# Attention A with 128 stationary columns: GpSimd's norm behind the splits, and z, xn and the projections in slots 10 to 15 of the preceding iteration

## The chip, the core and the metric

The kernel runs on one core of one Trainium2 chip. The metric is the device time of one execution in microseconds (us); smaller is better. TensorE is called PE below, VectorE DVE, ScalarE ACT, GpSimd POOL, and the queue of SyncE that issues the DMAs SP.

## What is computed

A small transformer on 32 sequences of 256 tokens of width 128, float32: attention A, a feed-forward layer, attention B, the feed-forward layer again. The program has three stages one after the other, `attention_a`, `dense` and `attention_b`. The change is in `attention_a` alone, which computes, for each sequence (a block):

```python
y  = layernorm(x)                                # the caller's norm
z  = layernorm(y)                                # attention A's own norm, before g1 and b1
xn = z * g1 + b1
q, k = lin(xn, Wq, bq) / sqrt(8), lin(xn, Wk, bk)   # 16 heads of 8
v  = lin(xn, Wv, bv)                             # 8 "rules" of 8, shared by all heads
out  = softmax(q @ k.T) @ v                      # per head, 256 x 256 scores
comp = softmax over rules([qv, out] @ Ws.T + bs)
ao   = sum over rules(comp * out)                # goes to DRAM, and y too
```

The scores are taken from bfloat16 operands that carry float32 precision: q and k are each split into three bfloat16 parts, and the 9 products of parts are stacked on 72 rows of the contraction. The row maxima of the scores (negated, again in three parts) are stacked as 24 more rows, so that a second matmul of the same operands gives the scores shifted by their maximum, transposed.

## The kernel before

`attention_a` is a software pipeline written out by hand: every engine runs `body(j, u)` for the iterations n = 2j + u, and in iteration n an engine works on several blocks at once, each with its lag. `active(j, u, lag)` asks whether block n - lag exists. The first six iterations and the last are unrolled, the others are a hardware loop of two iterations. The engines meet through semaphores only, and each executes its instructions strictly in the order of the code. PE and ACT split an iteration into 16 slots `s` (one head each); the order inside a slot is that of the code.

In iteration n, with the lines of the profile:

- SP loads x of block n+2, stores y of block n (L286), stores the parts of block n as soon as POOL has split them (L292), waits until they have landed in DRAM, and reads them back in two halves of 8 heads as stacked operands `q_st[i]` (L305) and `k_st[i]` (L308, three per half). Each half also waits until the shift matmuls of block n-2 no longer read that half of the buffer (`shifted`): half 0 until slot 4, half 1 until slot 12.
- PE: in slot 1 it transposes z of block n (L628), in slot 3 it projects q and k of block n (L647, L648), in slot 5 it projects v of block n-1 (L652), in slots 2 and 10 it transposes parts of the row maxima (L639). Every slot has two *shift* matmuls (L593, block n-1 from slot 13 on, block n-2 before), four *values* matmuls (L609, each two records), and the 16 score units of block n-1 (L578, two matmuls each) are spread by `S_AT` over slots 0 to 13, two units in slots 0 and 2. A score unit writes one of two PSUM banks, so unit w waits until DVE has reduced unit w-2 (`maxed`); unit 0 waits for the stacked operands of its half to land (`stack_in`), and so does unit 8 in slot 6. In iterations 1 to 4, slot 0 opens with `fold`, the product of two feed-forward weights that a later stage needs (L557 to L563).
- The shift matmul of head 8 of block n-2 stands in slot 5, that of head 0 of block n-1 in slot 13; each waits (`m_in`) until POOL has written 8 heads' rows of maxima into `q_st` (`spread`, L345).
- ACT: slot 2 copies transposed maxima (L470) and makes xn of block n (L473), slot 4 evicts q and k of block n from PSUM (L477, L479), slot 10 copies maxima (L488). Every slot has an exponential (L496) and every odd slot a copy of values (L505); slot 5 has another exponential (L511). At the end of slot 14 it makes y of block n+1 (L520, twice) and z of its first half (L525), at the end of slot 15 z of its second half.
- DVE reduces the score units (L697), and between them does the weighing of block n-3 (L772 to L782), the moments of block n+1 (L727, L731), the sums of block n-4 (L740), and the splitting of the maxima (L714, L716).
- POOL, in this order: `spread(1, n-2)` (L345), the subtraction of block n-3 (L360), the four splits of block n (L376 to L379, which wait for `qk_d`, ACT's eviction of slot 4), the first four instructions of the norm of block n+1 (L395 to L398), `spread(0, n-1)` (L345), the other four of the norm (L403 to L406), the four products of block n-3 (L416).

The bank `zv_ps` takes in turn the transposes of z, the projection of v and the folds, the bank `qk_ps` the projections of q and k and the transposed maxima (`mt_ps`); semaphores guard each reuse.

## Time and profile before

| | |
|---|---|
| median of 3 runs | 1583.43 us (1572.7 to 1587.1) |
| the profiled execution | 1586.89 us |
| its span | 1585.1 us |
| mean granted TensorE clock over the span | 0.933 |
| `attention_a` | from 0 to about 772 us of the span |
| its iterations, its blocks | n from -1 to 35, 32 |

The profile is of one execution. A row of the timeline is one instruction, or a run of equal ones where it ends in x2 or more; the bracket at its end tells how long the engine had been idle before it, and what ended that. Matmuls overlap, so the start of the next says more than the duration.

### The profile page before, as it was taken

What the parts mean: (1) busy time and instruction counts of PE and PEld (TensorE: products, weight loads), DVE (VectorE), ACT (ScalarE), POOL (GpSimd) and SP (SyncE); (2) the same over time, 40 slices, a digit from 0 to 9 for tenths busy, and PEclk for the clock granted to TensorE, in tenths of its full rate; (3) what the DMA queues carried; (4) which work ended last, traced back from release to release, by engine and by line L of the source; (5) the groups of instructions that cost most, each with busy time, mean ns of one, the idle gap of its engine ahead of it and who ended that gap; (6) DMA issues with size and microseconds to landing.
All of it is one profiled execution on the core that took longest, in us unless ns stands there. A gap on an engine that the chain in (4) does not pass through costs nothing. (4 is left out here: it accounts for less than half of the span.)

```text
span 1585.1 us, 52984 instructions
## 1 busy us (share of the span) xinstructions
PE 1328.7 (84%) x16996; PEld 1165.0 (73%) x16996; DVE 1095.4 (69%) x3074; ACT 873.5 (55%) x2020; POOL 927.5 (59%) x1340
## 2 busy tenths in 40 slices
PE   5999999999999999999477873787887778887786
PEld 4898998899888988999456652576666667666675
DVE  4467787788777887888344444667677777767874
ACT  2466766666666666676356652444454544444442
POOL 4456766667667666775478873445445554444551
PEclk9899999999999999999789995879799998879996
DMA  4523322332233223331144422434344444334331
GB/s 136 159 85 104 101 77 82 89 99 80 79 89 99 78 81 89 99 91 51 44 127 121 134 70 74 111 109 119 105 127 119 116 121 124 106 104 117 112 117 46
DMA packets 181701, 158.23 MB, mean 100 GB/s; under 512 B 12529, under 2 KB 163185, under 8 KB 181618
## 3 DMA queue, kind: packets, MB, share of 16 engines
q1 hardware_dynamic: 181618, 157.17, 35.1%
q8 instruction: 46, 0.75, 0.2%
q14 instruction: 37, 0.30, 0.1%
HBM read 113.09 MB, written 44.04 MB: 99 GB/s over the span
## 5 line engine op out<-in xcount | busy, mean ns | idle before, releaser
L609 PE MATMUL a_bank<-a_vp,a_prob 128*128 128x74 f32 x4096 | 598.0, 253 | 0.0
L609 PEld LDWEIGHTS a_bank<-a_vp,a_prob 128*128 128x128 f32 x4096 | 587.8, 192 | 5.5
L697 DVE TENSOR_REDUCE a_nmax<-a_bank 128x2 f32<-128x512 f32 x512 | 344.9, 685 | 156.9 <-PE a_bank L578 156.7
L496 ACT ACTIVATE a_prob<-a_bank 128x512 f32<-128x512 f32 x512 | 305.5, 597 | 216.0 <-PE a_bank L593 210.7
L578 PE MATMUL a_bank<-a_k_st,a_q_st 96*128 96x256 bf16 x1024 | 259.5, 276 | 38.3 <-DVE a_nmax L697 25.2
L593 PE MATMUL a_bank<-a_q_st,a_k_st 120*128 120x256 bf16 x1024 | 281.5, 275 | 2.2 <-POOL a_q_st L345 2.2
L416 POOL TENSOR_TENSOR a_prod<-a_ov,a_wgt 128x512 f32<-128x512 f32 x128 | 152.5, 1192 | 34.1 <-POOL a_prod L416 17.2
L345 POOL TENSOR_SCALAR a_q_st<-a_mt 24x2048 bf16<-24x2048 bf16 x64 | 121.5, 1898 | 82.6 <-ACT a_mt L470 36.9
L578 PEld LDWEIGHTS a_bank<-a_k_st,a_q_st 96*128 96x128 bf16 x1024 | 128.9, 134 | 50.0 <-DVE a_nmax L697 32.1
L1504 ACT ACTIVATE c_prob<-c_bank 128x256 f32<-128x256 f32 x256 | 98.8, 386 | 101.4 <-PE c_bank L1596 97.1
L593 PEld LDWEIGHTS a_bank<-a_q_st,a_k_st 120*128 120x128 bf16 x1024 | 140.1, 137 | 11.0 <-issue 2.6
L1647 PE MATMUL c_bank<-c_vb,c_prob 128*64 128x18 f32 x2048 | 109.3, 221 | 0.8 <-DVE c_ad L1919 0.8
L505 ACT COPY a_ov<-a_bank 128x292 f32<-128x292 f32 x256 | 101.5, 396 | 14.4 <-POOL a_prod L416 13.0
L1439 POOL TENSOR_SCALAR c_parts<-c_kq 128x512 bf16<-128x512 f32 x32 | 19.9, 621 | 147.9 <-ACT c_kq L1529 147.9
L1802 DVE TENSOR_REDUCE c_nmax<-c_bank 128x8 f32<-128x512 f32 x128 | 88.0, 687 | 20.6 <-PE c_bank L1616 19.4
L1574 PE MATMUL c_bank<-c_uv,c_skn 128*64 128x144 f32 x384 | 47.2, 326 | 63.9 <-DVE c_am L1840 62.8
L1647 PEld LDWEIGHTS c_bank<-c_vb,c_prob 128*64 128x64 f32 x2048 | 90.9, 151 | 7.2 <-issue 3.7
L1421 POOL TENSOR_SCALAR c_vb<-c_vs 64x128 f32<-64x128 f32 x128 | 39.0, 305 | 86.9 <-PE c_bank L1647 56.2
L1596 PEld LDWEIGHTS c_bank<-c_q_st,c_k_st 128*64 128x64 bf16 x2048 | 82.4, 121 | 6.7 <-issue 1.4
L1574 PE MATMUL c_bank<-c_late,c_pick 88*64 88x256 bf16 x512 | 80.3, 307 | 2.0 <-issue 2.0
L1596 PE MATMUL c_bank<-c_q_st,c_k_st 128*64 128x64 bf16 x2048 | 81.6, 204 | 0.0
L740 DVE TENSOR_REDUCE a_ao<-a_prod 128x128 f32<-128x1024 f32 x64 | 77.3, 1209 | 4.3 <-POOL a_prod L416 4.3
(205 smaller groups left out, 2821.2 us busy)
## 6 DMA issues: line engine op xcount, KB each, us to landing
a_q_st<-scratch_a_parts_dram SPq DMA_DIRECT2D x64, 288.0 KB
a_k_st<-scratch_a_parts_dram SPq DMA_DIRECT2D x192, 96.0 KB
c_q_st<-scratch_c_parts_dram SPq DMA_DIRECT2D x64, 288.0 KB
c_k_st<-scratch_c_parts_dram SPq DMA_DIRECT2D x192, 96.0 KB
scratch_a_parts_dram<-a_parts SPq DMA_DIRECT2D x32, 384.0 KB, 2.7
scratch_c_parts_dram<-c_parts SPq DMA_DIRECT2D x32, 384.0 KB, 2.7
a_x<-in_x SPq DMA_DIRECT2D x32, 128.0 KB, 3.5
scratch_y<-a_y SPq DMA_DIRECT2D x32, 128.0 KB, 3.1
```

What stands on the lines that cost most here:

```text
L345: pool.tensor_scalar(q_st[o][MROW:AROWS, hs, :], mt[half_][MROW:AROWS, :].unsqueeze(1).broadcast_to([AROWS - MROW, H // 2, T]), 1.0, 0.0, ...
L416: pool.tensor_tensor(prod[o][:, gs, :].rearrange("p g (e r) -> p g e r", r=R), ov[o][:, gs, 0:RD].rearrange("p g (e r) -> p g e r", r=R), ...
L496: act.activation(prob[h % 4][:, :, :].rearrange("p a b -> p (a b)"), t_ps[h % 2][:, :], ACT.Exp).then_inc(exped, 1)
L505: act.copy(ov[(i + lag) % 2][:, 4 * g:4 * g + 4, :], o_ps[g % 2][:, 0:4 * VC].rearrange("p (g c) -> p g c", g=4)[:, :, 0:CQ]).then_inc(ov_ ...
L578: mm = pe.matmul(s_ps[t][:, hh * T:(hh + 1) * T], q_st[o][0:MROW, 2 * g + hh, t * P:(t + 1) * P], k_st[o][0:MROW, 2 * g + hh, :], start=Tr ...
L593: mm = pe.matmul(t_ps[h % 2][:, c * T:(c + 1) * T], k_st[o][0:AROWS, h, c * P:(c + 1) * P], q_st[o][0:AROWS, h, :], start=True, stop=True)
L609: mm = pe.matmul(o_ps[g % 2][:, at:at + VM], prob[h % 4][:, c, t * P:(t + 1) * P], vp[o][:, c, 0:VM], start=c == 0, stop=c == NT - 1)
L697: dve.tensor_reduce(nmax[:, t, 2 * g:2 * g + 2, 0], s_ps[t][:, :].rearrange("p (h k) -> p h k", h=2), AX.X, ALU.max, negate=True).then_inc ...
L1504: act.activation(prob[g % 4][:, :], t_ps[g % 2][:, 0:T], ACT.Exp).then_inc(exped, 1)
L1574: mm = pe.matmul(out[cs, :], lhsT[:, cs], rhs, start=True, stop=True)
L1596: mm = pe.matmul(t_ps[g % 2][hh * SEG:(hh + 1) * SEG, cs], k_st[st][:, 2 * g + hh, cs], q_st[st][:, 2 * g + hh, cs], start=False, stop=Tru ...
L1647: mm = pe.matmul(o_ps[a * SEG:(a + 1) * SEG, at:at + VG], prob[g % 4][:, c * SEG:(c + 1) * SEG], vb[st][:, t, src:src + VG], start=True, s ...
```

## The change

On POOL the splits of block n come first in an iteration, ahead of `spread(1, n-2)` and the subtraction, and the eight instructions of the norm of block n+1 stand together ahead of `spread(0, n-1)`. What makes the input of the splits moves one stage back: in iteration n, block n+1 (not n) is transposed and projected. ACT makes y and z of block n+1 in slots 10 and 11 (before: 14 and 15), PE transposes z in slot 12 (before: slot 1 of the next iteration), ACT makes xn at the end of slot 13 (before: slot 2 of the next), PE projects q and k at the start of slot 15 (before: slot 3 of the next), and ACT evicts them first thing in slot 0 of the next iteration (before: slot 4 of it). Waits follow: the transposes of z wait for the newest v eviction (`v_d`), the projections for the newest copy of maxima of slot 10, the transposes of maxima of slot 2 (no longer those of slot 10) for the eviction of q and k, and a fold waits until xn has left the bank. No instruction is added or taken away apart from waits.

```diff
--- before.py
+++ after.py
@@ -220,6 +220,7 @@
         OFF, PVLAG = 13, 2
         S_AT = (0, 0, 1, 2, 2, 3, 4, 5, 6, 7, 8, 9, 10, 11, 12, 13)
         MT_AT = (10, 2)
+        Z_AT, ZT_AT, XN_AT, QK_AT = 10, 12, 13, 15
         PIECES, STAGES, FOLDED = 4, 5, 8
         N_LOAD, N_LOAD_V = 4, 8
         FOLD_AT = range(1, 1 + NG // 2)
@@ -350,6 +351,24 @@
             def body(j, u):
                 n = 2 * j + u
                 i = u
+                if active(j, u, 0):
+
+                    pool.wait_ge(qk_d, (n + 1) * 2)
+                    if not isinstance(j, int) or n >= 2:
+                        pool.wait_ge(parts_out, (n - 1) * 16)
+
+                    def split(k, ins):
+                        ins.then_inc(split_d, 1)
+                        pool.wait_ge(split_d, n * SPLIT + k)
+                        apart(pool, spare)
+
+                    apart(pool, spare)
+                    split(1, pool.tensor_scalar(parts[i][:, :, 0, :], qk[i][:, :, :], 1.0, 0.0, ALU.mult, ALU.add))
+                    split(2, pool.tensor_tensor(rest[:, :, :], qk[i][:, :, :], parts[i][:, :, 0, :], ALU.subtract))
+                    split(3, pool.tensor_scalar(parts[i][:, :, 1, :], rest[:, :, :], 1.0, 0.0, ALU.mult, ALU.add))
+                    split(4, pool.tensor_tensor(parts[i][:, :, 2, :], rest[:, :, :], parts[i][:, :, 1, :],
+                                                ALU.subtract))
+
                 if active(j, u, 2):
                     spread(1, n - 2, i)
                 if active(j, u, 3):
@@ -361,24 +380,6 @@
                                        cmax[:, :].unsqueeze(2).broadcast_to([P, H * NT, R]), ALU.subtract
                                        ).then_inc(post, 1)
                     pool.wait_ge(post, b * POST + 5)
-                if active(j, u, 0):
-
...
                 def norm(k, ins):
                     ins.then_inc(norm_d, 1)
                     pool.wait_ge(norm_d, (n + 1) * NORM + k)
@@ -396,14 +397,13 @@
                     norm(2, pool.tensor_tensor(r1[:, :], rt[:, 0, :], half[:, :], ALU.pow))
                     norm(3, pool.tensor_scalar(rt[:, 4, :], mv[:, :, 0], -1.0, None, ALU.mult))
                     norm(4, pool.tensor_tensor(shift[:, :], rt[:, 4, :], r1[:, :], ALU.mult))
-                if active(j, u, 1):
-                    spread(0, n - 1, 1 - i)
-                if active(j, u, -1):
                     apart(pool, spare)
                     norm(5, pool.tensor_tensor(rt[:, 1, :], r1[:, :], r1[:, :], ALU.mult))
                     norm(6, pool.tensor_tensor(rt[:, 2, :], rt[:, 1, :], mv[:, :, 1], ALU.mult))
                     norm(7, pool.tensor_scalar(rt[:, 3, :], rt[:, 2, :], EPS, None, ALU.add))
                     norm(8, pool.tensor_tensor(r2[:, :], rt[:, 3, :], half[:, :], ALU.pow))
+                if active(j, u, 1):
+                    spread(0, n - 1, 1 - i)
                 if active(j, u, 3):
 
                     b, o = n - 3, 1 - i
@@ -455,6 +455,12 @@
                 n = 2 * j + u
                 i = u
                 for s in range(H):
+                    if s == 0 and active(j, u, 0):
+                        act.wait_ge(qk_p, n + 1)
+                        act.activation(qk[i][:, 0, :], qk_ps[:, 0:T], ACT.Identity, scale=HD ** -0.5,
+                                       bias=b_qs[:, 0:1]).then_inc(qk_d, 1)
+                        act.activation(qk[i][:, 1, :], qk_ps[:, T:2 * T], ACT.Identity,
+                                       bias=cols[:, 1:2]).then_inc(qk_d, 1)
                     if s == 0 and isinstance(j, int) and n in FOLD_AT:
                         act.wait_ge(ffn_p, n)
                         if n > 2:
@@ -468,16 +474,6 @@
                         if not isinstance(j, int) or b >= 1:
                             act.wait_ge(m_in[1], b)
                         act.copy(mt[1][MROW:AROWS, :], mt_ps).then_inc(mt_d, 1)
-                    if s == 2 and active(j, u, 0):
-                        act.wait_ge(z_t, n + 1)
-                        act.activation(xn[i][:, :], zv_ps[:, 0:T], ACT.Identity, scale=cols[:, 2:3],
-                                       bias=cols[:, 3:4]).then_inc(xn_d, 1)
-                    if s == 4 and active(j, u, 0):
-                        act.wait_ge(qk_p, n + 1)
-                        act.activation(qk[i][:, 0, :], qk_ps[:, 0:T], ACT.Identity, scale=HD ** -0.5,
-                                       bias=b_qs[:, 0:1]).then_inc(qk_d, 1)
-                        act.activation(qk[i][:, 1, :], qk_ps[:, T:2 * T], ACT.Identity,
-                                       bias=cols[:, 1:2]).then_inc(qk_d, 1)
                     if s == 9 and isinstance(j, int) and n == 0:
                         values_weights()
                     if s == MT_AT[0] and active(j, u, 1):
@@ -509,9 +505,9 @@
                         b = n - 3
                         act.wait_ge(post, b * POST + 5)
                         act.activation(cexp[:, :, :], comp3[:, :, :], ACT.Exp).then_inc(cexp_d, 1)
-                    if s >= H - NT and active(j, u, -1):
-
-                        t = s - H + NT
+                    if Z_AT <= s < Z_AT + NT and active(j, u, -1):
+
+                        t = s - Z_AT
                         if t == 0:
                             act.wait_ge(norm_d, (n + 2) * NORM)
                             if not isinstance(j, int) or n >= 1:
@@ -524,6 +520,11 @@
                             act.wait_ge(z_t, n)
                         act.activation(z[1 - i][:, t, :], y[1 - i][:, t, :], ACT.Copy, scale=r2[:, t:t + 1]
                                        ).then_inc(z_d, 1)
+
+                    if s == XN_AT and active(j, u, -1):
+                        act.wait_ge(z_t, n + 2)
+                        act.activation(xn[1 - i][:, :], zv_ps[:, 0:T], ACT.Identity, scale=cols[:, 2:3],
+                                       bias=cols[:, 3:4]).then_inc(xn_d, 1)
 
             pipeline(act, body, stages=STAGES, ahead=1)
 
@@ -613,25 +614,24 @@
 
                 for s in range(H):
                     if s == 0 and isinstance(j, int) and n in FOLD_AT:
+                        pe.wait_ge(xn_d, n + 1)
                         if n > 1:
                             pe.wait_ge(v_d, n - 1)
                         fold(n - 1)
                     if s == 9 and isinstance(j, int) and n == 0:
                         values_weights()
-                    if s == 1 and active(j, u, 0):
-                        if isinstance(j, int) and n in FOLD_AT:
-                            pe.wait_ge(ffn_d, n)
-                        pe.wait_ge(z_d, (n + 1) * NT)
-                        if not isinstance(j, int) or n >= 2:
-                            pe.wait_ge(v_d, n - 1)
+                    if s == ZT_AT and active(j, u, -1):
+                        pe.wait_ge(z_d, (n + 2) * NT)
+                        if not isinstance(j, int) or n >= 1:
+                            pe.wait_ge(v_d, n)
                         for t in range(NT):
-                            mm = pe.transpose(zv_ps[:, t * P:(t + 1) * P], z[i][:, t, :], ident[:, :])
+                            mm = pe.transpose(zv_ps[:, t * P:(t + 1) * P], z[1 - i][:, t, :], ident[:, :])
                         mm.then_inc(z_t, 1)
                     for half_ in range(2):
                         if s == MT_AT[half_] and active(j, u, half_ + 1):
                             b = n - half_ - 1
                             pe.wait_ge(mp_d, b * MP + MP // 2 * (half_ + 1))
-                            if half_ == 0:
+                            if half_ == 1 or isinstance(j, int):
                                 pe.wait_ge(qk_d, min(n + 1, NB) * 2 if isinstance(j, int) else (n + 1) * 2)
                             if half_ or not isinstance(j, int) or b >= 1:
                                 pe.wait_ge(mt_d, 2 * b + half_)
@@ -640,14 +640,16 @@
                                                   mpart[:, t, half_, :, :].rearrange("p a h -> p (a h)"),
                                                   ident16[:, :])
                             mm.then_inc(mt_p, 1)
-                    if s == 3 and active(j, u, 0):
-                        pe.wait_ge(xn_d, n + 1)
-                        if not isinstance(j, int) or n >= 2:
-                            pe.wait_ge(mt_d, 2 * (n - 1))
-                        pe.matmul(qk_ps[:, 0:T], w_q[:, :], xn[i][:, :], start=True, stop=True)
-                        pe.matmul(qk_ps[:, T:2 * T], w_k[:, :], xn[i][:, :], start=True, stop=True).then_inc(qk_p, 1)
+                    if s == QK_AT and active(j, u, -1):
+                        pe.wait_ge(xn_d, n + 2)
+                        if not isinstance(j, int) or n >= 1:
+                            pe.wait_ge(mt_d, 2 * n - 1)
+                        pe.matmul(qk_ps[:, 0:T], w_q[:, :], xn[1 - i][:, :], start=True, stop=True)
+                        pe.matmul(qk_ps[:, T:2 * T], w_k[:, :], xn[1 - i][:, :], start=True, stop=True).then_inc(qk_p, 1)
                     if s == 5 and active(j, u, 1):
                         pe.wait_ge(xn_d, min(n + 1, NB) if isinstance(j, int) else n + 1)
+                        if isinstance(j, int) and n in FOLD_AT:
+                            pe.wait_ge(ffn_d, n)
                         for t in range(NT):
                             mm = pe.matmul(zv_ps[:, t * VC:(t + 1) * VC], xn[1 - i][:, t * P:(t + 1) * P], w_v[:, :],
                                            start=True, stop=True)
```

## Rows read from the trace of the kernel before

**Rows 1.** Windows: busy of PE, PEld, DVE, ACT, POOL; PEclk, DMA share, GB/s

```profile
600.00:700.00 100.00, 95.17 (x918) 90.84 (x918) 80.99 (x182) 68.18 (x154) 69.89 (x84) 1.00 0.29 86
```

**Rows 2.** Waits, 200 to 760 us: us in total, times, longest

```profile
PE a_bank L578 <- DVE a_nmax L697: 18.8, 26, 0.9
...
PE a_bank L578 <- DMA a_k_st<-scratch_a_parts_dram: 9.1, 14, 1.2
```

**Rows 3.** The line of xn, 150 to 720 us: duration in ns, first and last start

```profile
L473 ACT ACTIVATE a_xn<-a_bank,a_cols x26: 564/564/565, 151.9 to 715.2; 128x256 f32<-128x256 f32 x26
```

**Rows 4.** Timeline of PE, one iteration: start, us, what, xcount [idle before <-releaser]

```profile
215.53 0.27 PE L593 MATMUL a_bank<-a_q_st,a_k_st 120*128 120x256 bf16 x1
...
216.50 0.39 PE L578 MATMUL a_bank<-a_k_st,a_q_st 96*128 96x256 bf16 x2 [0.23 <-DMA a_k_st<-scratch_a_parts_dram]
...
217.31 0.38 PE L628 MATMUL a_bank<-a_ident,a_z 128*128 128x128 f32 x2
217.52 0.27 PE L593 MATMUL a_bank<-a_q_st,a_k_st 120*128 120x256 bf16 x1
...
220.86 0.39 PE L578 MATMUL a_bank<-a_k_st,a_q_st 96*128 96x256 bf16 x2 [0.73 <-DVE a_nmax L697]
...
221.27 0.64 PE L647 MATMUL a_bank<-a_xn,a_w_q 128*128 128x256 f32 x2
...
222.18 0.28 PE L593 MATMUL a_bank<-a_q_st,a_k_st 120*128 120x256 bf16 x1
...
224.96 0.28 PE L593 MATMUL a_bank<-a_q_st,a_k_st 120*128 120x256 bf16 x1
...
231.06 0.28 PE L593 MATMUL a_bank<-a_q_st,a_k_st 120*128 120x256 bf16 x1
...
233.39 0.27 PE L593 MATMUL a_bank<-a_q_st,a_k_st 120*128 120x256 bf16 x1
...
236.74 0.27 PE L593 MATMUL a_bank<-a_q_st,a_k_st 120*128 120x256 bf16 x1
...
237.76 0.27 PE L593 MATMUL a_bank<-a_q_st,a_k_st 120*128 120x256 bf16 x1
```

**Rows 5.** Timeline of ACT: end of the iteration before, and slot 10

```profile
214.16 0.60 ACT L496 ACTIVATE a_prob<-a_bank 128x512 f32<-128x512 f32 x1 [0.27 <-PE a_bank L593]
...
216.47 0.41 ACT L525 ACTIVATE a_z<-a_y,a_r 128x128 f32<-128x128 f32 x1
...
231.67 0.60 ACT L496 ACTIVATE a_prob<-a_bank 128x512 f32<-128x512 f32 x1
```

**Rows 6.** Timeline of DVE, the start of the same iteration

```profile
218.01 0.42 DVE L773 TENSOR_TENSOR a_comp<-a_ov,a_inv 128x256 f32<-128x256 f32 x1
...
218.95 0.80 DVE L774 TENSOR_TENSOR a_comp<-a_comp,a_vp 128x256 f32<-128x256 f32 x1
...
220.13 1.28 DVE L697 TENSOR_REDUCE a_nmax<-a_bank 128x2 f32<-128x512 f32 x2
```

**Rows 7.** Timeline of POOL, the same iteration

```profile
220.57 1.90 POOL L345 TENSOR_SCALAR a_q_st<-a_mt 24x2048 bf16<-24x2048 bf16 x1 [1.09 <-ACT a_mt L470]
222.72 0.63 POOL L360 TENSOR_TENSOR a_comp<-a_comp,a_cmax 128x256 f32<-128x256 f32 x1 [0.26 <-POOL a_q_st L345]
224.75 0.62 POOL L376 TENSOR_SCALAR a_parts<-a_qk 128x512 bf16<-128x512 f32 x1 [1.40 <-ACT a_qk L479]
...
229.32 0.22 POOL L395 TENSOR_SCALAR a_rt<-a_mv 128x2 f32<-128x2 f32 x1 [0.45 <-POOL a_parts L379]
...
236.26 1.18 POOL L416 TENSOR_TENSOR a_prod<-a_ov,a_wgt 128x512 f32<-128x512 f32 x1 [0.41 <-POOL a_r L406]
```

**Rows 8.** Timeline of SP, the same iteration

```profile
228.97 0.38 SPq L292 DMA_DIRECT2D scratch_a_parts_dram<-a_parts  x1
```

**Rows 9.** Timeline of PE at the start: iterations 0 and 1

```profile
20.21 2.08 PE L557 MATMUL a_bank<-a_w 128*128 128x128 f32 x8 [0.91 <-ACT a_b_v L452]
...
28.80 0.61 PE L578 MATMUL a_bank<-a_k_st,a_q_st 96*128 96x256 bf16 x4 [1.79 <-DMA a_k_st<-scratch_a_parts_dram]
```

19 lines of the change are left out of this document (9 added, 10 removed).

## The prediction

> **What bounds the kernel now.** I read the windows first, to see which engine is full; then the waits, for what still stops that engine; then the timeline of one iteration, engine by engine, because the change moves work between slots and everything depends on who is on time for whom.
>
> In the hardware loop PE is busy 95.17 of 100 us at a granted clock of 1.00, DVE 80.99, POOL 69.89, ACT 68.18 [rows 1]. So PE bounds `attention_a`, and only its stalls can be had. It has two [rows 2]. Wait A, 9.1 us in 14 iterations: the first score unit of slot 0 stands until the stacked operands land. Wait B, 18.8 us in 26: the second score unit of slot 2 stands until DVE has reduced the unit two before it. The 25 periods from iteration 6 on average (715.2 - 151.9) / 25 = 22.53 us [rows 3].
>
> Let S be the start of an iteration's first shift on PE. The iteration shown runs from 215.53 to 237.76, 22.23 us [rows 4]. A stall costs more than the idle time shown, since matmuls overlap: the transposes of z are given 0.38 us but the next starts 0.21 after them, so 0.17 goes on top. A cost 0.23 + 0.17 = 0.40, B 0.73 + 0.17 = 0.90; without both the iteration is 20.93 us of pure PE work. Its pieces [rows 4]: z transposes 0.21, projections of q and k 222.18 - 221.27 = 0.91, slots 10 and 11 together 233.39 - 231.06 = 2.33, slot 15 1.02. The rest of the mean, 22.53 - 20.93 = 1.60, is A and B over all iterations: B about 1.0, A about 0.6.
>
> **The change, part by part.**
>
> 1. *Wait A goes.* Before, the projections start at S + 5.74 and POOL's first split at S + 9.22 (224.75), 3.48 later [rows 4, 7]; the parts are stored at 228.97 [rows 8], S + 13.44, and the stacked operands land just when the next slot 0 wants them or after. Now the projections stand before slot 15, 0.91 + 1.02 = 1.93 before the next S. With the same 3.48 (an exponential, a copy and the two evictions stand between, as before) the splits start at S + 1.55 and the store follows 4.2 later, at about S + 5.8, 7.6 us sooner. Half 0 also waits for the shift of slot 4, which is over by about S + 7; half 1 waits for slot 12, about S + 18, and is wanted only in slot 6 of the next iteration. Both have several us in hand. Gain 0.6 a steady iteration, at most; below it, nothing is left to gain in A. SP's other issues (x, y, ao) keep their place and are late for nobody.
>
> 2. *Wait B grows.* Its DVE chain starts with the score unit of slot 0, at 216.50, and lets PE go at 220.86, 4.36 later [rows 4]. B costs 0.90, so PE was ready 3.46 after the score. Transposing z in slot 1 was thus free, hidden in B. Without it PE is ready 0.21 sooner, at 3.25, and B is 1.11 if the chain keeps its length. In slot 12 the same 0.21 is paid in full. The projections of slot 3 come after B and are in the sum either way: nothing for the 0.91. Can the chain shorten? The second of DVE's two additions on SBUF operands took 0.80 and the first 0.42 [rows 6], because POOL's last product was still running. Now the products end about 2.3 us sooner (the second half of the norm no longer stands between `spread(0)` and them), but the splits, from S + 1.55, take their place: the second one runs from about S + 2.4 to S + 3.5 and the second addition would start at S + 3.0. I keep 4.36; the ends are 3.96 (no meeting) and 4.6 (both additions held).
>
>    The Trainium skill ("SBUF — State Buffer", section "SBUF: two separate sides") has a rule for this: DVE with two SBUF operands and GpSimd take a shared port pair as an exclusive lock for the whole instruction. The trace agrees (0.80 against 0.42); by the rule B stays 1.1, and by the rows alone it could be 0.7, which item 3 gives back.
>
> 3. *`spread(1)` comes after the splits.* Before, it ran at 220.57 for 1.90 [rows 7], and the shift of slot 5, which waits for it, ran at 224.96: 2.5 us in hand. Now the splits take 229.32 - 224.75 = 4.57 [rows 7] from S + 1.55, the spread ends at S + 8.02 and PE may go at S + 8.1. PE itself gets to that shift at 224.96 - 215.53 = 9.43, less A 0.40, B 0.90, z 0.21 and projections 0.91, which is S + 7.01, plus the new B 1.11: S + 8.12. The slack is gone to the hundredth: B and this wait together are at least 1.1. So the gain of a shorter DVE chain could not be had, and each tenth by which POOL is later costs PE a tenth. I take 0; the bound above is 0.6 (POOL held by both of DVE's additions).
>
> 4. *A new wait, D, in slot 12.* This decides. In slot 14 of before, ACT's exponential starts at 214.16 and its second z, with y twice, z, the next exponential and a copy of values between, starts at 216.47 and ends at 216.88: 2.72 us [rows 5]. Nobody minded: the transposes came at 217.31. Now the same sequence starts with the exponential of slot 10, which follows its shift by 231.67 - 231.06 = 0.61 [rows 4, 5], so the second z is ready 0.61 + 2.72 = 3.33 after slot 10 starts, and PE hears of it 0.09 later (the delay from DVE's end, 220.13 + 0.64, to PE's start, 220.86). But PE reaches the transposes, at the head of slot 12, 2.33 after slot 10 starts. It stands 3.42 - 2.33 = 1.09 us, every iteration. Behind the waiting instruction stand the shift, score and value matmuls of slots 12 to 15: all of PE, and nothing makes up for it, as PE has no other slack. Below: 0.9 (start of the last z earlier by a copy's overlap); above: 1.3 (weights of the transposes can't be loaded ahead of z). Is r2 on time for y? The norm takes 236.26 - 229.32 less one spread with its gap (2.1), 4.8 us [rows 7]; it starts after the spread (S + 8.0) and the subtraction (1 us with its gaps), so it ends by S + 13.9; y wants it at S + 7.01 + 1.11 + the 6.1 from 224.96 to 231.06 + 0.61 + 0.49 = S + 15.3. In time, by 1.4 us.
>
> 5. *xn and the projections.* xn stands after slot 13's exponential and copy; start 1.4 after that slot begins, 0.56 long [rows 3], ready at about 2.1, where slots 13 and 14 last 2.2. It is hidden, by 0.1 us only. ACT's evictions at the head of slot 0 delay its exponential by 0.6, and the next use of it is two slots on: nothing.
>
> 6. *The start.* Before, the first fold (20.21 to about 27.0) ran on PE while the second block's norm was made, and the first scores began at 28.80, when their operands landed [rows 9]. Now iteration 0 holds the second block's z and projections, made when the norm lets them, at 26 to 29 us, and the fold stands behind them: 29 to about 35, all exposed. 6 us later; about 1.5 comes back because iteration 1 no longer waits for z and projections in its first slots while POOL splits late. I take +4.6, ends 0 and +7.
>
> 7. *Iterations 2 to 5* have no or little A, and B only from 3 on: D 4 x 1.09, plus B 3 x 0.21, less A 0.55 in the last: +4.4. *Iteration 31* has no z and projections any more: -0.9.
>
> **Sum.** Steady iterations 6 to 30: 20.93 + 1.11 + 1.09 = 23.13 against 22.53, +0.60, x 25 = +15.0. With +4.6, +4.4 and -0.9: +23.1 us. On the profiled execution's 1586.89 that is 1610; it lies 3.5 above the median of the runs shown, so between 1606.5 and 1610. How much of A a run of before has depends on when DMAs land, and the new kernel has no A; so I go by the profile: 1610 us.
>
> **Rivals.**
>
> - *The chain of z is covered* (D is 0): ACT's sequence would have to be under 2.33 - 0.09 - 0.61 = 1.63 us long instead of 2.72, or PE to lose a microsecond elsewhere in slots 10 and 11. Nothing in the rows says so, but 30 x 1.09 = 32.7 hang on one place. Time 1610 - 32.7 = 1577; 1563 to 1592 with the fill and B at their ends. Not slower. It decides where the second z lands within 2.24 us of slot 10's start. 0.22.
> - *POOL is late with the spread.* From an added 0.6 us for each of 27 iterations, +16: 1626. For it: no slack at all at S + 8.1. Against it: POOL is busy only 70 of 100 us. 0.08.
> - *Forecast*, D as worked out: 0.70, own range 1598 to 1626.
>
> About 1%, 16 us, is what a measurement of this kernel can tell from no change; its runs spread by 14 us. The covered case gives faster 0.07 (under 1568) and same 0.15; of the forecast 0.03 lies within 1% (no loss at the start). So faster 0.07, same 0.18, slower 0.75. The range 1585 to 1630 leaves out most of the covered case below and the latest POOL above.
>
> **What would show it.** The waits should have a new line, PE's transposes (L628's successor) waiting for ACT's z, about 0.9 us shown x 30, and none of PE for the DMA of `a_k_st`. The wait for DVE's reduction stays, 0.9 shown. The period of xn's line becomes 23.1. The store of parts stands 5.8 us behind S. If PE's shift of slot 5 waits for POOL's `a_q_st`, item 3 was too kind. The first scores begin near 35 us. I am wrong if ACT's second z is done before PE's slot 12, or if the loop's period is under 22.5.

## The result and the profile after

| | before | after |
|---|---|---|
| median | 1584.12 us (4 runs, 1572.7 to 1587.1) | 1618.69 us (4 runs, 1612.23 to 1622.82) |
| ratio after / before | | 1.0228, 95% interval 1.0165 to 1.0291 |
| the profiled execution | 1586.89 us | 1612.23 us |
| its span, mean granted clock | 1585.1 us, 0.933 | 1610.4 us, 0.935 |

The change makes the kernel slower, by 2.3%; the interval lies wholly above 1, and leaves open whether the loss is more or less than 2%. Each ratio compares the executions in a kernel's usual state alone, since some show a lower granted clock and a longer time whatever the kernel, so it is not quite the quotient of the medians. From profile to profile the difference is 25.3 us, from median to median 34.6. To see where it arises, take the first instruction of the stage `dense` on POOL, which stands for the end of `attention_a`. The first fence is the timeline of POOL of before, the second that of after (start, us, instruction, in brackets the idle time before it).

```profile
784.18 0.10 POOL L955 MEMSET b_half<- 128x4 f32 x1 [4.84 <-POOLq L98]
```

```profile
811.75 0.10 POOL L957 MEMSET b_half<- 128x4 f32 x1 [4.84 <-POOLq L98]
```

`attention_a` ends 27.6 us later (prediction: 23.1). What follows is the same code, 800.9 us before (1585.1 - 784.2) and 798.7 after. So, between these two executions, the whole loss is in the stage that was changed.

**The waits.** PE's waits from 200 to 760 us of after: us in total, times, longest.

```profile
PE a_bank L579 <- DVE a_nmax L699: 22.0, 24, 0.9
PE a_bank L628 <- ACT a_z L521: 20.6, 23, 0.9
```

Against [rows 2], the wait for the DMA of the stacked operands is gone, the wait for DVE's reduction is 0.92 each instead of 0.72, and a new line stands beside them: the transposes of z wait 0.90 for ACT, 23 times. The window of after that answers to [rows 1] (busy of PE, PEld, DVE, ACT, POOL; clock):

```profile
600.00:700.00 100.00, 91.81 (x885) 87.61 (x884) 76.95 (x178) 65.08 (x147) 65.67 (x81) 1.00 0.28 83
```

In this window PE lost 3.4 of 100 us, and over the five such windows from 200 to 700 us 2.4 on average (94.6 busy before, 92.2 after). The clock is 1.00 as before: nothing here runs slower, PE stands more. xn's line of after, against [rows 3]:

```profile
L526 ACT ACTIVATE a_xn<-a_bank,a_cols x25: 581/581/581, 155.2 to 713.7; 128x256 f32<-128x256 f32 x25
```

24 periods of (713.7 - 155.2) / 24 = 23.27 us; over iterations 6 to 30 the mean is 23.26, against 22.53.

**One iteration**, PE's timeline of after, to be laid beside [rows 4]. It starts at S = 320.98.

```profile
320.98 0.27 PE L594 MATMUL a_bank<-a_q_st,a_k_st 120*128 120x256 bf16 x1
...
321.56 0.38 PE L579 MATMUL a_bank<-a_k_st,a_q_st 96*128 96x256 bf16 x2
...
325.89 0.39 PE L579 MATMUL a_bank<-a_k_st,a_q_st 96*128 96x256 bf16 x2 [0.92 <-DVE a_nmax L699]
...
329.08 0.28 PE L594 MATMUL a_bank<-a_q_st,a_k_st 120*128 120x256 bf16 x1
...
335.20 0.28 PE L594 MATMUL a_bank<-a_q_st,a_k_st 120*128 120x256 bf16 x1
...
338.59 0.44 PE L628 MATMUL a_bank<-a_ident,a_z 128*128 128x128 f32 x2 [0.90 <-ACT a_z L521]
338.86 0.27 PE L594 MATMUL a_bank<-a_q_st,a_k_st 120*128 120x256 bf16 x1
...
342.21 0.67 PE L647 MATMUL a_bank<-a_xn,a_w_q 128*128 128x256 f32 x2
...
343.15 0.27 PE L594 MATMUL a_bank<-a_q_st,a_k_st 120*128 120x256 bf16 x1
...
344.18 0.27 PE L594 MATMUL a_bank<-a_q_st,a_k_st 120*128 120x256 bf16 x1
...
352.34 0.28 PE L594 MATMUL a_bank<-a_q_st,a_k_st 120*128 120x256 bf16 x1
```

The score unit of slot 0 no longer waits. Slot 10 starts at 335.20 and the transposes at the head of slot 12 run 3.39 later, where slots 10 and 11 alone last 2.33 [rows 4]: the new wait costs 1.06 us of the iteration. ACT's timeline of after says what it is for, against [rows 5]:

```profile
335.81 0.60 ACT L492 ACTIVATE a_prob<-a_bank 128x512 f32<-128x512 f32 x1
336.31 0.87 ACT L516 ACTIVATE a_y<-a_x,a_shift,a_r 128x128 f32<-128x128 f32 x2
...
338.13 0.41 ACT L521 ACTIVATE a_z<-a_y,a_r 128x128 f32<-128x128 f32 x1
```

There is no idle time in brackets: ACT works through its own list, and the second z, which PE needs, is the last of it, 2.73 us after the exponential of slot 10 began (338.13 + 0.41 - 335.81); PE starts 0.05 later. POOL's timeline of after, against [rows 7]: the first split, `spread(1)`, and the last instruction of the norm.

```profile
322.54 0.62 POOL L366 TENSOR_SCALAR a_parts<-a_qk 128x512 bf16<-128x512 f32 x1 [2.29 <-ACT a_qk L462]
...
327.08 1.90 POOL L346 TENSOR_SCALAR a_q_st<-a_mt 24x2048 bf16<-24x2048 bf16 x1 [0.43 <-PE a_bank L594]
...
333.57 0.72 POOL L404 TENSOR_TENSOR a_r<-a_rt,a_half 128x2 f32<-128x2 f32 x1 [0.18 <-POOL a_rt L403]
```

### The profile page after: what moved, and what is told of

Its sections match the earlier page's. It is cut to its first block and busy times, and to the rows that moved or that the text cites. A ratio compares the mean times of both kernels' runs of the same rounds, so it can differ in the third digit from the quotient of the medians.

```text
span 1610.4 us, 52987 instructions
## 1 busy us (share of the span) xinstructions
PE 1330.1 (83%) x16996; PEld 1165.6 (72%) x16996; DVE 1100.7 (68%) x3074; ACT 870.3 (54%) x2020; POOL 919.2 (57%) x1340
```

## The experiments

"Stage end" is the start of `dense` as above (before 784.2, after 811.7), "period" the mean of iterations 6 to 30 (22.53 and 23.26). These two show a change of `attention_a` more sharply than the median does, because the rest of the program, the same code in all kernels, takes 779.1 (e9) to 831.0 us from one profiled execution to the next (831.0 is e1's, whose profiled execution, 1628.96 us, is the longest of its five; e9's, 1545.64, is the shortest of its ten). Each ratio is to executions of before that were taken beside it, with medians of 1576.14 us (e1, e2, e3, e5), 1579.80 (e4, e6, e8) and 1582.16 (e9, e10), and not to the 1584.12 above.

| kernel | built on | stage end | period | median | ratio to before (95%) |
|---|---|---|---|---|---|
| e6_z_together | after | 790.3 | 22.50 | 1592.28 | 1.0075 (1.0040 to 1.0111) |
| e1_z_slot9 | after | 796.2 | 22.81 | 1602.53 | 1.0138 (1.0076 to 1.0199) |
| e2_z9_dve_order | e1 | 792.8 | 22.65 | 1613.35 | 1.0210 (1.0138 to 1.0282) |
| e3_z9_dve_pool | e2 | 832.1 | 23.94 | 1623.62 | 1.0283 (1.0225 to 1.0342) |
| e10_reduce3_first | e3 | 798.0 | 22.82 | 1598.38 | 1.0153 (1.0042 to 1.0263) |
| e5_spread_first | after | 827.2 | 23.85 | 1632.04 | 1.0362 (1.0285 to 1.0438) |
| e7_fold_early | after | 808.0 | 23.26 | 1614.48 (one run) | - |
| e8_before_norm_whole | before | 805.9 | 22.99 | 1607.66 | 1.0127 (1.0054 to 1.0199) |
| e4_before_dve_order | before | 769.3 | 22.02 | 1556.90 | 0.9857 (0.9806 to 0.9908) |
| e9_chain_earlier | e4 | 764.8 | 21.81 | 1562.84 | 0.9908 (0.9866 to 0.9950) |

**e6_z_together: is the new wait the length of ACT's list?** Both halves of z are made in slot 10, one after the other, so that no exponential and no copy stand between them. Work, engine order and POOL stay as in after.

```diff
-                    if Z_AT <= s < Z_AT + NT and active(j, u, -1):
-                        t = s - Z_AT
+                    for t in range(NT) if s == Z_AT and active(j, u, -1) else ():
```

> The changed kernel with ACT's second z made right behind the first, in slot 10, not in slot 11. Nothing else moves: unlike e1_z_slot9, where y and z of slot 9 pushed the copy of maxima of slot 10 back by 0.7 us and with it POOL's spread and products, that copy is ahead of them here. Theory (D is ACT's sequence against PE's 2.33 us): without an exponential and a copy of values between the two z, the second is ready 0.61 + 0.49 + 0.77 + 0.29 + 0.41 + 0.09 = 2.66 after slot 10 starts, and D falls from 1.09 to 0.3. The period falls from 23.26 to 22.5, attention_a ends at 789 to 792 us instead of 811.7. The wait for DVE stays at 0.92 shown. Rival (POOL's full order, not ACT's, holds the period): it stays above 23.

Measured: stage end 790.3, period 22.50. Of PE only the wait for DVE is left from 200 to 760 us (22.6 us in 25); the waits of PEld have this line:

```profile
PEld a_bank L626 <- ACT a_z L519: 6.0, 23, 0.3
```

The wait of the transposes is gone from PE and only 0.3 us of PE's weight loading is left; the wait for DVE is as long as in after. This one edit takes back 21.4 of the 27.6 us. So item 4 of the prediction is shown: what is lost is the time by which ACT's list ends behind PE's slot 12, and nothing else of the move costs much. The kernel is then even with before in its period, with a start that is still longer.

**e1_z_slot9: the whole list one slot sooner.**

```diff
-        Z_AT, ZT_AT, XN_AT, QK_AT = 10, 12, 13, 15
+        Z_AT, ZT_AT, XN_AT, QK_AT = 9, 12, 13, 15
```

> The changed kernel with one number changed: y and z of the next block start in slot 9, not 10; everything else stays. Theory (wait D: PE stands 0.9 us in front of the transposes of z in every one of 30 iterations because ACT's second z is late): with one slot more in hand the wait for ACT's z disappears from PE's waits, the period of the loop falls from 23.27 to about 22.2 us, and the time by 30 x 1.09 = 33 us, to about 1580 to 1586, no different from the kernel before within 1%. Wait B, 0.92 shown, stays as it is. POOL's norm ends at S + 13.3 and y is wanted at S + 13.9, so it is still in time. Rival 1 (the loss is due to POOL's new order, or to the exposed fold at the start): the time stays near 1612 to 1619, whatever becomes of the wait. Rival 2 (the wait only moves to xn or the projections): the wait for ACT shows up at L647 instead and less than 10 us are gained.

Measured: 15.5 us back where 33 were expected. The wait for z is gone, but the other grew: 25.8 us in 25, up to 1.24. Four rows of the timeline (ACT, POOL, DVE) around an iteration that starts at 472.94 tell most of it:

```profile
466.03 0.36 ACT L484 COPY a_mt<-a_bank 24x256 bf16<-24x256 bf16 x1
...
473.00 1.18 POOL L416 TENSOR_TENSOR a_prod<-a_ov,a_wgt 128x512 f32<-128x512 f32 x1 [0.18 <-POOL a_prod L416]
474.98 0.62 POOL L366 TENSOR_SCALAR a_parts<-a_qk 128x512 bf16<-128x512 f32 x1 [0.80 <-ACT a_qk L462]
...
475.02 0.85 DVE L775 TENSOR_TENSOR a_comp<-a_ov,a_inv 128x256 f32<-128x256 f32 x1
```

The two DVE instructions that the prediction calls additions (L775, L776) are, by the code, a multiplication and an addition, of the same shape and both with operands in SBUF; "additions" means both here too. y and z now stand ahead of the copy of maxima on ACT, `spread(0)` starts 0.28 us behind that copy, and POOL's products end at S + 1.24, where in after they ended 0.73 before S. The splits follow at S + 2.04, and DVE's first addition, which was free at S + 2.08 in after, is held too (0.85 instead of 0.42). That is so in every second iteration only: in the one that starts at 495.81 the first split stands 0.37 us behind the products and not 0.80, at S + 1.61, the first addition is free (0.42), and PE waits 0.96 and not 1.24. Two such iterations are one pass of the hardware loop; what the 0.43 us are that its first iteration has more, no run takes apart. The expectation had ACT's slot as free; it was not, as ACT is in order as well.

There is a second part. Behind four of its waits of 1.24 us the granted clock fell, to 0.50 for about 3 us, and these four periods are 24.33 us where the others of their kind are 22.87. They add 5.9 us (4 x 1.46, an estimate from these periods); without them the stage would end at about 790.

**e2_z9_dve_order: the reduction that PE waits for goes ahead of DVE's two additions.** e1, and on DVE:

```diff
-                reduces(0, 1)
+                reduces(0, 2)
                 weighs(0, 2)
-                reduces(1, 2)
-                weighs(2, 4)
                 reduces(2, 3)
+                weighs(2, 4)
```

> As e1_z_slot9, and DVE reduces the second and third score units before the second addition and the maximum of the weighing: reduces(0,2), weighs(0,2), reduces(2,3), weighs(2,4). Theory (item 3 of the prediction: wait B and the wait for POOL's spread at the shift of slot 5 are together at least 1.1 us, because the spread ends at S + 8.0 and PE would be there at S + 7.0): the idle time before L579 that DVE ends falls from 0.92 to under 0.2 an iteration, a new wait of PE's L594 for POOL's a_q_st appears, about 0.9 to 1.0 shown, and the time stays that of e1_z_slot9 within 5 us. Rival (there is room at slot 5, B is a loss of its own): no wait for POOL, period 21.2, 25 to 30 us less than e1_z_slot9.

Measured: stage end 792.8, 3.4 us less than e1. That is not a gain of the edit: e2's clock is 1.00 all through the loop, and e1 without its four falls of the clock would stand at about 790. Waits of PE and, from its timeline, a shift of slot 5:

```profile
PE a_bank L579 <- DVE a_nmax L699: 15.5, 37, 0.6
PE a_bank L594 <- POOL a_q_st L346: 9.7, 11, 0.9
```

```profile
480.64 0.28 PE L594 MATMUL a_bank<-a_q_st,a_k_st 120*128 120x256 bf16 x1 [0.88 <-POOL a_q_st L346]
```

What DVE gives, POOL takes in every second iteration (11 waits in about 25): with the splits ahead of it, `spread(1)` ends when PE would have come anyway. In the other ones DVE's first addition meets a split (1.16 us) and PE still waits for reductions, 0.51 and 0.23. So DVE's wait fell to 0.62 an iteration and not below 0.2 as expected, and the time stayed where e1's was. That agrees with item 3 of the prediction ("B and this wait together are at least 1.1"). The median, 1.0210, says less for this kernel: in its profiled execution the last stage, the same code in every kernel, had a granted clock of 0.82 (below).

**e3_z9_dve_pool: then let `spread(1)` come between the second and third split.** e2, and on POOL:

```diff
                     split(2, pool.tensor_tensor(rest[:, :, :], qk[i][:, :, :], parts[i][:, :, 0, :], ALU.subtract))
+                if active(j, u, 2):
+                    spread(1, n - 2, i)
                     split(3, ...)
                     split(4, ...)
-                if active(j, u, 2):
-                    spread(1, n - 2, i)
```

> As e2_z9_dve_order, and on POOL the spread of half 1 stands between the second and the third split instead of behind the fourth. Theory: the spread now starts at S + 3.9 and ends at S + 5.8, before PE is at the shift of slot 5 (S + 7.0), so wait B and the wait for POOL are both gone. The next limit is the norm, which still ends at S + 13.3 while y in slot 9 is wanted at S + 12.8 by the faster PE: a wait of 0.2 to 0.5 us for ACT's z comes back in slot 12. Period about 21.4, 20 to 25 us less than e1_z_slot9, about 1560. Rival (something else, DVE or the landing of the stacked operands, sets a period of 22.2 anyway): the time stays within 5 us of e1_z_slot9 and the waits of PE name it.

Measured: 1623.62, the expectation (some 1560) missed by a long way. Rows of the timeline (POOL, DVE, PE), and the window behind the last of them (width, busy of PE, PEld, DVE, ACT, POOL, clock):

```profile
472.01 1.90 POOL L346 TENSOR_SCALAR a_q_st<-a_mt 24x2048 bf16<-24x2048 bf16 x1 [0.43 <-POOL a_rest L367]
472.39 1.79 DVE L779 TENSOR_TENSOR a_comp<-a_comp,a_vp 128x256 f32<-128x256 f32 x1
...
475.29 0.32 PE L582 MATMUL a_bank<-a_k_st,a_q_st 96*128 96x256 bf16 x1 [1.61 <-DVE a_nmax L702]
```

```profile
475.00:478.40 3.40, 3.11 (x18) 3.12 (x19) 3.06 (x8) 0.60 (x1) 2.51 (x4) 0.56 0.37 112
```

DVE's addition began while the spread was on and took 1.79 us instead of 0.42; it ended 0.27 after the spread. The reduction queued behind it came late, PE stood 1.61 us, and in the stretch after that the granted clock was 0.56 (1.00 in the 15 us before), near the lower of its two levels (1.2 of 2.4 GHz). Both add up: the period is 23.94. The clock's part is the larger. Two of the waits of 1.61 us, at 237.89 and 333.51, left the clock at 1.00, and their periods are 23.65 and 23.66; where it fell they are 25.1 to 26.9. The eleven periods of that kind, each less 23.66, make 21 us (an estimate). Moving the long POOL instruction onto DVE's additions was worse than leaving it late.

**e10_reduce3_first: is it that one reduction?** e3, and on DVE the fourth reduction too goes ahead of the second addition:

```diff
-                reduces(2, 3)
+                reduces(2, 4)
                 weighs(2, 4)
                 for k in range(2 * NT):
-                    if k % 2 == 0:
-                        reduces(3 + k // 2, 4 + k // 2)
+                    if k == 2:
+                        reduces(4, 5)
```

> e3_z9_dve_pool with one thing changed: DVE also reduces the fourth score unit before its second addition. In e3 that addition started at 472.39 while POOL's spread ran from 472.01 to 473.91, took 1.79 us instead of 0.42, and PE stood 1.61 us for the reduction behind it; right after, the granted clock was at its lower level (1.2 GHz) for 3.4 us. Theory (the addition is held by the spread; what PE loses is the reduction queued behind it, and the clock's fall is its consequence): with the fourth reduction ahead of the addition the 1.6 us wait goes, the clock stays at 1.00 in the loop, the period falls from 23.94 to 21.9 to 22.4, attention_a ends at 785 to 793 us instead of 832; the addition still shows about 1.7 us. Rival (the spread's place between the splits, or the clock by itself, is what costs): period above 23.

Measured: stage end 798.0 against 832.1 of e3, 34 us back by a change of DVE's order alone. Waits of PE, and DVE's second addition in its timeline (the first took 1.19 as well):

```profile
PE a_bank L582 <- DVE a_nmax L702: 20.8, 38, 0.8
PE a_bank L631 <- ACT a_z L524: 12.1, 11, 1.1
```

```profile
456.86 1.19 DVE L779 TENSOR_TENSOR a_comp<-a_comp,a_vp 128x256 f32<-128x256 f32 x1
```

The long wait is gone, and the granted clock is 1.00 in every 100 us of 200 to 700 (e3: 0.95 to 0.98). The mechanism of e3 is shown: the reduction behind the held addition made the long wait, and with that wait the falls of the clock went too, some 21 of the 34 us. But in every second iteration the additions are still held, three times as long as alone, and the smaller waits they leave (0.85 for the fifth reduction, which now stands behind them), with z late again every second iteration, hold the period at 22.82 where 21.9 to 22.4 was expected. I had counted the one wait away and not those behind it.

**e5_spread_first: POOL's old head order.** after, with `spread(1)` and the subtraction ahead of the splits:

```diff
+                if active(j, u, 2):
+                    spread(1, n - 2, i)
+                if active(j, u, 3):
+                    ... subtraction of block n-3
                 if active(j, u, 0):
                     ... splits 1 to 4
-                if active(j, u, 2):
-                    spread(1, n - 2, i)
-                if active(j, u, 3):
-                    ... subtraction of block n-3
```

> The changed kernel with POOL's old order at the head of an iteration (spread of half 1, subtraction, then the splits), the norm still in one piece. Theory: the norm ends 2 us later, at S + 15.9 instead of S + 13.3, while y in slot 10 is wanted at S + 15.3, so wait D grows from 0.90 to 1.3 to 1.6 shown; in return no split runs beside DVE's second addition, which takes 0.42 instead of 0.78, and wait B falls from 0.92 to 0.55 shown. Together 0.1 to 0.4 more an iteration: 0 to 12 us slower than the changed kernel. Rival (the new order of POOL is what costs the time of the change): 15 us or more faster than the changed kernel. Rival 2 (DVE's addition is not held by POOL's splits): B stays 0.92 and the loss is 15 to 20 us.

```profile
PE a_bank L628 <- ACT a_z L521: 37.2, 24, 1.6
PE a_bank L579 <- DVE a_nmax L699: 13.2, 24, 0.6
```

The sizes are those expected: the additions of DVE run free, and the wait for its reduction shrinks from 0.92 to 0.56; the norm comes later on POOL, so y and z do, and the wait for z grows from 0.90 to 1.56. The total, 1632, is above what was expected (the stage ends 15.5 us later, for 0 to 12), and part of it is again the clock: 0.98 instead of 1.00 through the loop, with a period of 24.8 to 25.1 every fourth time against 23.47 otherwise. These 23.47 are 0.21 above after's 23.26, within the 0.1 to 0.4 expected; the six longer ones add some 9 us. Splits first is thus right for after: the norm is what the new chain hangs on.

**e7_fold_early: the start.** after, with the first fold back in iteration 0, ahead of the second block's z (its semaphores follow):

```diff
-                    if s == 0 and isinstance(j, int) and n in FOLD_AT:
+                    if s == 0 and isinstance(j, int) and n in FOLD_AT and n > 1:
                         ...
+                    if s == 10 and isinstance(j, int) and n == 0:
+                        fold(0)
```

> The changed kernel with the first fold in iteration 0, where PE waits 6.6 us for z of the second block, and not behind the projections in iteration 1. Theory (item 6: the fold is exposed at the start): the first scores begin at about 31 us instead of 35.4, the stage ends 4 to 5 us sooner (807), the steady period stays 23.26. Rival (the start is bound by POOL's or ACT's chain and not by PE): the stage ends at 811 as before.

Measured: first scores at 31.61 instead of 35.37, stage end 808.0, so 3.8 us back (4 to 5 expected), all of it at the start and with the period unchanged at 23.26. The exposed fold is shown as a cost of its own; it is also the cheap part of the loss to undo.

**e8_before_norm_whole: the norm in one piece, alone.** before, with the last four instructions of the norm ahead of `spread(0)`:

```diff
                     norm(4, ...)
-                if active(j, u, 1):
-                    spread(0, n - 1, 1 - i)
-                if active(j, u, -1):
                     apart(pool, spare)
                     norm(5, ...) to norm(8, ...)
+                if active(j, u, 1):
+                    spread(0, n - 1, 1 - i)
```

> One part of the change alone: the kernel before, with POOL's norm in one piece ahead of the spread of half 0, everything else where it was. Theory (the norm was split around the spread because PE's shift of slot 13 waits for it): the spread of half 0 ends 2.1 us later, at 213.7 on the clock of the iteration shown, where slot 13 starts at 212.3, so PE gets a wait of about 1.3 us for POOL's a_q_st in slot 13; POOL's products end at the same time as before. Period 22.53 + 1.3 less what wait A gives back (0.6): 23.2 to 23.8, the stage ends 18 to 35 us later than 784. Rival (the wait is covered): period unchanged.

```profile
PE a_bank L592 <- POOL a_q_st L345: 28.1, 23, 1.2
```

Measured: +21.8 us at the stage end, within the 18 to 35 expected. The period, 22.99, lies under the 23.2 to 23.8 that were expected: DVE's second addition runs free (0.41 to 0.42 us instead of 0.80), and PE's wait for the reduction falls from 18.8 us to 6.0, which the expectation had not counted. Here PE's shift of slot 13 waits for `spread(0)`, which after does not do (there POOL itself sits idle 1.66 us for PE before that spread). So the parts of the change need each other: with the norm in one piece in before, PE waits for a spread; with the input of the splits early, as in after, it does not (nor in e5, which has that input early and the splits behind `spread(1)`).

**e4_before_dve_order: DVE's order without the rest.** before, with e2's edit on DVE and nothing else.

> The kernel before, with DVE's order of e2_z9_dve_order alone (the second and third score units reduced before the second addition and the maximum). Theory: B is not worth more than what the next chain leaves. Here the shift of slot 5 has 2.5 us in hand, so B may go; but the chain from the projections of slot 3 to the landing of the stacked operands (17.5 us, plus 3.9 from the score of slot 0 to slot 3) keeps the period at 21.4 to 22.2, and wait A takes part of what B gives. Stage attention_a ends at 765 to 780 us instead of 784, period 21.9 to 22.2. Rival (DVE's additions meet POOL's products for as long wherever they stand): period stays 22.5, the stage ends at 784.

Waits of PE from 200 to 760 us, and DVE's timeline at the start of an iteration, against [rows 2] and [rows 6]:

```profile
PE a_bank L578 <- DMA a_k_st<-scratch_a_parts_dram: 8.4, 11, 1.5
PE a_bank L578 <- DVE a_nmax L697: 4.6, 12, 0.4
```

```profile
238.57 1.29 DVE L697 TENSOR_REDUCE a_nmax<-a_bank 128x2 f32<-128x512 f32 x2 [2.45 <-PE a_bank L578]
...
241.10 0.41 DVE L774 TENSOR_TENSOR a_comp<-a_comp,a_vp 128x256 f32<-128x256 f32 x1
```

The wait for DVE falls from 18.8 us to 4.6, the second addition, later now than POOL's products, takes 0.41 instead of 0.80, and the stage ends 14.9 us sooner. Here `spread(1)` has 2.5 us in hand [rows 4, 7], so nothing takes the gain back, as it did in e2. The kernel is faster than before, by less than 2% (0.9857, interval 0.9806 to 0.9908), and faster than after. Of the 22.9 us between its median and that of before, 14.9 stand in `attention_a`; in the profiled execution the rest of the program, the same code, took 784.8 us and not 800.9, which the edit does not explain.

**e9_chain_earlier: and the wait for the DMA?** e4, with xn, the projections and their eviction each one slot sooner (slots 1, 2, 3), the transposes of maxima of slot 2 moved to 1, and e10's edit on DVE:

```diff
-        MT_AT = (10, 2)
+        MT_AT = (10, 1)
...
-                    if s == 2 and active(j, u, 0):      # ACT: xn
+                    if s == 1 and active(j, u, 0):
...
-                    if s == 4 and active(j, u, 0):      # ACT: evictions
+                    if s == 3 and active(j, u, 0):
...
-                    if s == 3 and active(j, u, 0):      # PE: projections
+                    if s == 2 and active(j, u, 0):
```

> A candidate, from the kernel before with DVE's order of e4: the chain to the splits moves only one slot forward (transposes of maxima in slot 1, xn at the head of ACT's slot 1, projections in slot 2, their eviction in slot 3), z, y and POOL's order stay, and DVE reduces the third and fourth unit too before the second addition. Theory: what is left in e4_before_dve_order (period 22.02 against 20.93 of pure work) is wait A, 0.4 to 1.5 us; with the projections 1.2 to 2 us earlier the operands land before slot 0 asks for them. The spread of half 1 now runs beside DVE's second addition and holds it up for up to 1.9 us, but no reduction that PE waits for stands behind it. Period 21.2 to 21.6, attention_a ends at 748 to 760 us instead of 769. Rival (the held-up addition or ACT's fuller slot 1 takes the gain back): period 21.9 or more.

```profile
PE a_bank L578 <- DVE a_nmax L697: 12.6, 23, 1.2
PE a_bank L578 <- DMA a_k_st<-scratch_a_parts_dram: 0.9, 1, 0.9
```

The wait for the DMA is all but gone with a move of one slot, where after moved the whole chain an iteration back. The stage ends 4.4 us before that of e4, short of the 748 to 760 expected, and the period is 21.81 for 21.2 to 21.6, because DVE's wait came back at 0.55 each. Two rows of DVE's timeline show where:

```profile
456.42 0.92 DVE L774 TENSOR_TENSOR a_comp<-a_comp,a_vp 128x256 f32<-128x256 f32 x1
...
458.10 0.68 DVE L697 TENSOR_REDUCE a_nmax<-a_bank 128x2 f32<-128x512 f32 x1
```

`spread(1)` runs from 455.17 to 457.07, the second addition is held until 457.34, and the fifth reduction, which now stands behind it, lets PE go at 458.83 after a wait of 0.74. The expectation had no reduction behind it that PE waits for. The median, 1562.84, is not below that of e4; which of the two is better stays open.

## The prediction, point by point

The direction was right, and so was the mechanism; the start was put too low. The median lies 8.7 us above the forecast, within the range.

1. *Wait A goes*: right. No wait for the DMA is left. Its size was a remainder: the text gave A 0.6 and B 1.0 of the 1.60 us, where [rows 2] with 0.17 on each wait make 0.46 and 0.93 over the 24.9 iterations of that window. The forecast does not hang on this split, as it adds up from 20.93. The first split stands at 322.54, S + 1.56 (1.55 in the text), the parts are stored at 326.75, S + 5.77 (5.8), by SP's timeline of after:

```profile
326.75 0.38 SPq L293 DMA_DIRECT2D scratch_a_parts_dram<-a_parts  x1
```

2. *Wait B grows*: right. From the score unit at 321.56 to 325.89 it is 4.33 us (4.36), with 0.92 shown. The two additions, by DVE's timeline of after, are as the text chose between its ends:

```profile
323.06 0.42 DVE L775 TENSOR_TENSOR a_comp<-a_ov,a_inv 128x256 f32<-128x256 f32 x1
...
324.01 0.78 DVE L776 TENSOR_TENSOR a_comp<-a_comp,a_vp 128x256 f32<-128x256 f32 x1
```

The first falls about between POOL's first two splits, the second meets the second split (323.34, for 1.16) and is held. The rule of the Trainium skill ("SBUF — State Buffer", section "SBUF: two separate sides"), that DVE with two SBUF operands and GpSimd exclude one another for a whole instruction, agrees with this and with e3's 1.79: the held addition ended at 324.79, 0.29 us after the second split, and e3's 0.27 after the spread.

3. *No slack at slot 5*: right. The spread ended at S + 8.00 (8.02), the shift ran at S + 8.10 (8.12). In the next iteration, which starts at 344.18, it ran at 352.34, S + 8.16: POOL set it there, and that iteration is 0.14 us longer from there on. e2 showed that shortening wait B gains nothing while POOL stands there.

4. *The new wait D*: right, 1.06 us of an iteration (1.09), and e6 shows the cause. ACT's list took 2.73 us from the exponential (2.72). The norm ended at S + 13.31 (by 13.9 in the text), y began at S + 15.33 (15.3).

5. *xn and the projections are hidden*: right in the loop; the projections at 342.21 carry no wait.

6. *The start*: the term was mis-sized. The text took +4.6 us with ends 0 and +7. Rows of PE's timeline at the start of after, against [rows 9]:

```profile
35.37 0.61 PE L579 MATMUL a_bank<-a_k_st,a_q_st 96*128 96x256 bf16 x4
...
47.09 0.69 PE L628 MATMUL a_bank<-a_ident,a_z 128*128 128x128 f32 x2 [0.87 <-ACT a_z L521]
...
53.27 1.10 PE L558 MATMUL a_bank<-a_w 128*128 128x128 f32 x8
```

   The first scores at 35.37 are where the text put them. But the 1.5 us that were to come back did not: in iteration 1 PE waits for the third block's z at 47.09, and the second fold, at 53.27, stands 6.7 us behind that of before. The same row of before's timeline:

```profile
46.53 1.79 PE L557 MATMUL a_bank<-a_w 128*128 128x128 f32 x7
```

   The step that failed is that D was counted from iteration 2 on; iteration 1 has it as well, for 0.87 + 0.17 = 1.04 of the 2.1 us missed (an estimate, as the 0.17 is from rows at full clock). The rest of them was not taken apart. One part may be the clock: from 40 to 50 and from 50 to 60 us it was 0.50 and 0.85 in after, 0.59 and 1.00 in before.

7. *The steady part*: 23.26 against the 23.13 of the sum. The 0.13 are small things: the transposes of z take 0.27 after a wait (338.59 to 338.86) where the text had 0.21, the projections 0.94 (342.21 to 343.15) for 0.91, the 0.14 at slot 5 of every second iteration are 0.07 on average, and D is 0.03 less. Over 25 iterations that makes (23.26 - 22.53) x 25 = 18.3 us for 15.0. Together: 6.7 + 18.3 = 25.0, and 2.6 remain for iterations 2 to 5 and 31 (3.5 in the text), 27.6 in all.

The rivals: the covered chain, 1577, is refuted by the wait of L628 and, as its counter-test, by e6, in which the chain is nearly covered and the period falls to before's. The late spread, 1626, did not come to pass in after beyond 0.14 us in every second iteration, but e2 shows that it stood next in line.

Not shown: why the median lies 6.5 us above after's own profiled execution, while that of before lies 2.8 below its own. The runs above it have a lower mean clock over the span, but there is no profile of their stages.

## What to carry to other kernels

Before a step is moved to a quieter slot, set the end of the producer's in-order list (here ACT's, 2.73 us) against the time at which the consumer gets there (PE's, 2.33 us less what comes ahead): a transfer that stalled about half a microsecond an iteration was exchanged for a producer that stalls 1.06, and work that was free under another wait (the 0.21 of the transposes) was paid in full. When a wait is shortened, look for who would be late next; the same DVE edit gave 14.9 us where the next one had 2.5 us in hand (e4), and nothing of its own where it had none (e2). The gain that was to be had lay in reductions, which PE waits for, put ahead of two additions, which it does not wait for. And a stall of over a microsecond can cost twice: in e3 the falls of the clock behind such waits cost more than the waits.

## What the runs showed of the hardware

- One VectorE multiplication or addition, 128x256, of two SBUF operands: 0.41 to 0.43 us alone, 0.78 to 0.85 beside splits or products of GpSimd in before and after, 1.16 to 1.24 in e2, e3 and e10, and 1.79 in e3 beside GpSimd's 1.90 us copy. What decides is when the GpSimd instruction ends: in before, after, e1, e2, e3, e9 and e10 the held one shown ended 0.27 to 0.29 us after it. I had counted on tenths; it was enough to stop TensorE for 1.61 us.
- TensorE's granted clock stayed at 1.00 in a loop with waits of 0.92 and 0.90 us every 23 us (after) and with 0.8 and 1.1 (e10). With waits of 1.56 and 1.61 us it was 0.98 (e5) and 0.95 to 0.98 (e3), and 0.56 in the 3.4 us behind one of them. But the length of the single wait does not settle it alone: in e5 the clock fell in one of four iterations with the same wait, in e3 two waits of 1.61 left it at 1.00, and waits of 1.24 us were followed by a fall four times in e1 and never in the loop of e8, which has one in each iteration. What does stays open. A fall cost some 1.5 us of an iteration (24.33 for 22.87 in e1, 25.28 for 23.66 in e3).
- The last stage, the same code in every kernel, differs by 50 us between the profiled executions: from about 604 us at a clock of 0.90 (e9) to 654 at 0.82 (e1). Before it took 625 us at a clock of 0.87. Its window of after and of e2, whole stage each (width, busy of PE, PEld, DVE, ACT, POOL, clock):

```profile
988.00:1610.00 622.00, 483.46 (x9472) 387.56 (x9472) 449.19 (x1450) 280.85 (x711) 288.45 (x527) 0.88 0.38 110
```

```profile
970.00:1616.00 646.00, 515.36 (x9472) 411.49 (x9472) 452.71 (x1450) 281.14 (x711) 289.01 (x526) 0.82 0.37 105
```

  PE's busy time moves with its clock, 483 us at 0.88 and 515 at 0.82, with the same instructions. A change of the first stage that is worth less than this is read from that stage's own end, not from the total.
